# When the first six weight tiles of a fused Mamba and MLP kernel are loaded, and which products fill the second scan's norms

## The reference, cut to what matters

```python
h = patches @ W.T + b                       # tokens, 512 wide
x1 = layernorm(h)
r = x1 + mamba(rmsnorm(x1) * rms1_w)        # see below
r = r + down(silu(gate(n)) * up(n))         # n = rmsnorm(r) * rms2_w, hidden 2048
h = h + r
h = h + down2(silu(gate2(m)) * up2(m))      # m = layernorm(h), hidden 2048

# mamba, over the 10 tokens of one series, 1024 channels x 16 states:
z, xv, B, C, dt_in = split(x @ in_proj_w.T)
dt = softplus(dt_in @ dt_proj_w.T + dt_proj_b)
s[t] = exp(dt[t] * A) * s[t-1] + dt[t] * x[t] * B[t]
y[t] = sum over states of C[t] * s[t]
out = ((y + D_skip * x) * silu(z)) @ out_proj_w.T
```

## Time and profile before

| | |
|---|---|
| median of 3 runs | 665.3 us (664.75 to 665.99) |
| the profiled execution | 665.3 us, of which 663.5 us span |
| first scan, units 0 to 31 | about 30 to 203 us of the span |
| second scan, units 32 to 63 | about 203 to 440 us |
| outputs and MLPs of chunk 1 | from about 440 us |

### The profile page before, as it was taken

One profiled execution on the slowest core, in us unless ns is written; L12 is line 12 of the kernel. 1 busy time (PEld: TensorE's weight loads), 2 busy tenths in 40 slices (PEclk: granted clock), 3 DMA queues, 4 the chain that ended last, 5 costly groups with the idle time before them and its releaser, 6 DMA issues.

```text
span 663.5 us, 8621 instructions
## 1 busy us (share of the span) xinstructions
PE 627.1 (95%) x2846; PEld 501.8 (76%) x2846; DVE 416.9 (63%) x531; ACT 341.9 (52%) x768; POOL 429.0 (65%) x244
## 2 busy tenths in 40 slices
PE   5779998999995999999998999999999999999998
PEld 4547665666663767777765777766999998999998
DVE  4097887998877899888898888842232222332232
ACT  4368987488985564333374433413543443643440
POOL 0376766476777999987789987544465563455461
PEclk9959999999998999999999999999999999999999
DMA  8899996599999779988969998544244344244421
GB/s 334 305 372 344 304 328 231 189 356 347 329 362 395 279 250 367 412 332 308 323 223 312 402 326 315 171 127 159 96 133 151 103 154 127 66 144 136 131 68 44
DMA packets 49164, 163.50 MB, mean 246 GB/s; under 512 B 4320, under 2 KB 18528, under 8 KB 48480
## 3 DMA queue, kind: packets, MB, share of 16 engines
q1 hardware_dynamic: 49120, 162.95, 70.5%
HBM read 145.24 MB, written 17.69 MB: 246 GB/s over the span
## 4 chain that ended last, share of the span: by engine, by line
PE 76%; DVE 13%; issue 4%; ACT 3%; DMA 2%; POOL 1%; DVEq 0%; SPq 0%; ACTq 0%; POOLq 0%
PE work L1013 54%; PE da L1013 16%; DVE da L799 7%; PE work L1023 6%; DVE hs L809 3%; ACT L535 1%; DMA b_rows<-sq 1%; ACT da L561 1%; DMA bb<-b_rows 1%; DVE sq L883 1%; DMA sm<-small 1%; POOL hs L460 0%; DVE work L824 0%; DVE sq L899 0%; DVE a L892 0%
## 5 line engine op out<-in xcount | busy, mean ns | idle before, releaser
L799 DVE TENSOR_TENSOR_SCAN da<-da,hs 128x580 f32<-128x580 f32 (+1 forms) x128 | 191.1, 1493 | 35.0 <-POOL hs L460 19.2
L460 POOL TENSOR_TENSOR hs<-dtx,bb 128x1160 f32<-128x1160 f32 (+1 forms) x64 | 171.3, 2677 | 58.1 <-PE work L1023 43.7
L439 POOL TENSOR_TENSOR ws<-wraw,ws 128x1024 fp32r<-128x1024 f32 x40 | 101.3, 2534 | 92.9 <-ACT ws L570 92.9
L1013 PE MATMUL work<-sq,wraw 128*128 128x290 f32 x512 | 127.0, 407 | 3.8 <-DVE gate L952 2.6
L1013 PEld LDWEIGHTS work<-sq,wraw 128*128 128x128 f32 x512 | 96.1, 189 | 34.4 <-issue 4.8
L561 ACT ACTIVATE da<-dt,a_neg 128x261 f32<-128x261 f32 (+1 forms) x256 | 118.3, 494 | 0.0
L809 DVE TENSOR_TENSOR hs<-da,cb 128x580 f32<-128x580 f32 (+1 forms) x128 | 105.3, 823 | 15.3 <-DMA cb<-c_rows 6.8
L1013 PE MATMUL work<-hn,win 128*128 128x290 f32 (+1 forms) x336 | 98.7, 442 | 12.3 <-ACT c_rows L644 6.9
L1013 PEld LDWEIGHTS work<-hn,win 128*128 128x128 f32 x336 | 63.7, 192 | 41.9 <-issue 16.3
L558 ACT COPY da<-zeros 128x58 f32<-128x58 f32 (+1 forms) x128 | 27.7, 217 | 128.8 <-DVE hs L809 128.6
L570 ACT CAST ws<-wraw 128x1024 fp32r<-128x1024 f32 x48 | 50.3, 1049 | 70.4 <-PE da L1013 34.4
(11 more groups left out here) (103 smaller groups left out, 645.5 us busy)
## 6 DMA issues: line engine op xcount, KB each, us to landing
wraw<-w_stream SPq DMA_DIRECT2D x104, 512.0 KB, 4.0
bb<-b_rows SPq DMA_DIRECT2D x32, 700.0 KB, 7.5
cb<-c_rows SPq DMA_DIRECT2D x32, 700.0 KB, 5.9
bb<-b_rows SPq DMA_DIRECT2D x32, 580.0 KB, 8.5
cb<-c_rows SPq DMA_DIRECT2D x32, 580.0 KB, 6.7
c_rows<-c_rows SPq DMA_DIRECT2D x8, 875.0 KB, 10.6
c_rows<-c_rows SPq DMA_DIRECT2D x8, 725.0 KB, 7.1
win<-w_in SPq DMA_DIRECT2D x4, 1024.0 KB, 13.8
```

Of the source, the lines that this page charges most:

```text
L439: nc.gpsimd.tensor_tensor(ws[:, k % NW, 1, :], wraw[:, split_loads[k] % NRAW, :], ws[:, k % NW, 0, :].bitcast(F32), ALU.subtract).then_inc ...
L460: nc.gpsimd.tensor_tensor(hs[:, u % NH, 0:NQ * n].rearrange("p (n t) -> p n t", t=n), dtx[:, t % 2, 0:n].unsqueeze(1).to_broadcast([P, NQ, ...
L799: nc.vector.tensor_tensor_scan(da[:, j, 0:w], da[:, j, 0:w], hs[:, u % NH, j * w:(j + 1) * w], 0.0, ALU.mult, ALU.add).then_inc(scan_done, 1)
L1013: last = nc.tensor.matmul(dst, w, x, start=(k == 0), stop=(k == len(pairs) - 1))
```

## The change

Three things are changed. (1) The six first loads have a place each (`FIRST_LOADS`: the step beside which SP issues it, and the product that it waits for). Counted in units as SP reaches them: `wraw` 0 at unit 15, then 17, 18, 19, 24 and 25; before, all at unit 28. (2) `in_c` of tile 5 leaves unit 27 and is the filler ahead of `rms2`, in unit 36; `in_c` of tile 6 moves to the place behind `rms2`, which `in_z` of tile 7 had; and `in_z` of tile 7 goes to unit 33, ahead of the four outputs. (3) ACT loads the table with Tanh in the slots of `rms2` and `ln2_var`, at their end, where after `ln2_var` it was loaded just ahead of the first Tanh.

```diff
+FIRST_LOADS = [(("dtp", 0, 7), ("mean", 1)), (("in_x", 1, 1), ("in_x", 1, 0)), (("in_b", 1, 0), ("in_x", 1, 1)),
+               (("in_b", 1, 1), ("in_c", 1, 0)), (("in_z", 1, 0), ("in_z", 1, 0)), (("in_c", 1, 2), ("in_c", 1, 2))]
...
-    in_c = [("in_c", c, k) for k in (m, m + 1) if (c, k) != (0, 1)]
+    in_c = [("in_c", c, k) for k in (m, m + 1) if (c, k) not in ((0, 1), (1, 5))]
...
-    first = [[], [("xs", 1, 7)], o[0:2], o[2:4]]
+    first = [[], [("xs", 1, 7), ("in_z", 1, 7)], o[0:2], o[2:4]]
...
-        rest += {"rms2": [("in_c", 1, 6), s, ("in_z", 1, 7)], "ln2_mean": [s, ("dtp", 1, 7)],
+        rest += {"rms2": [("in_c", 1, 5), s, ("in_c", 1, 6)], "ln2_mean": [s, ("dtp", 1, 7)],
...
-SEAM = (("in_c", 1, 6), ("in_z", 1, 7), ("dtp", 1, 7), ("in_c", 1, 7))
+SEAM = (("in_c", 1, 5), ("in_c", 1, 6), ("dtp", 1, 7), ("in_c", 1, 7))
...
-                if i == 0:
-                    full(sp, ("in_z", 1, 2))
+                if i < NRAW:
+                    full(sp, FIRST_LOADS[i][1])
...
-                    if s == ("in_z", 1, 2):
-                        for i in range(NRAW):
+                    for i, (at, _) in enumerate(FIRST_LOADS):
+                        if s == at:
                             load_w(i)
...
                 if tables[0] == "silu_and_others" and unit is not None:
-                    use_tables("exp_and_others" if ("rms2", 0) in steps else "natural_log_exp_and_others")
+                    log_tables()
+                if ("rms2", 0) in steps or ("ln2_var", 0) in steps:
+                    if unit is not None:
+                        use_tables("exp_and_others")
```

## The result

The changed kernel takes 661.68 us (median of 6, 660.14 to 662.53) against 665.12 us beside it: ratio 0.9942, 95% interval 0.9928 to 0.9957, so 3.4 us less. The forecast was 662.3 us. Two later comparisons, on two chips, gave 0.9937 (0.9916 to 0.9957) and 0.9948 (0.9934 to 0.9962). The profiled execution took 661.63 us, of which 659.7 us span, 3.8 us less than the span before.

What follows compares the result with a forecast made beforehand. PE's chain was taken as the bound, held by a late last `y_done` as a load burst delayed DVE's rows. From 665.3 us, -4.0 + 1.3 + 0.6 - 0.95 = -3.05 us gave 662.3 us, range 659.0 to 665.6.

Steps and rivals of the forecast that it cites:

- The burst bounds the first scan's end: Near 200 us: six loads at once delay rows of C; without the burst the last `y_done` comes 4.0 us earlier.
- DVE keeps the whole of the 6.7 us: First scan's end: DVE gains all 6.7 us of its waits for C rows, giving 658.3 us; chance 0.13.
- the queue stays the bound: Up to the last `y_done`: rows still late by 2 to 3 us, about 664.8 us, no change; chance 0.17.
- `in_c` of tile 5 carries 0.7 us of it: First scan's end: removing this product from ahead of `in_z` carries about 0.7 of the 4.0 us gain.
- The early loads lose 1.3 us: Near 150 us: 3.8 us of backlog against 2.5 us of slack makes DVE wait 1.3 us for rows.
- The bounds of the step, 0 to 6.3: Early loads: 0 if DVE waits for ACT there anyway, 6.3 us if no slack covers anything.
- The second output waits 0.6 us longer: Outputs of chunk 0: its bank now awaits ACT's copy of the last `xs`, 6.6 us after `y_done`; 0.6 us lost.
- the clock gives nothing back, as PE waits for the bank instead: Outputs: 2.4 GHz held longer on PE gains 0 us, since the second output waits for its bank.
- The table at `ln2_var` gives 0.95 us: Seam at `ln2_var`: loading the table earlier, in ACT's idle time, brings Tanh, DVE and PE 0.95 us earlier.
- The store near 250 us costs nothing: Near 250 us: one more 875 KB store costs nothing, as rows have 4 us of lead against 3 us.
- The early loads cost more than they save: 126 to 180 us: five loads each hold the scan 1.3 us, giving 667.3 us, slower; chance 0.10.
- the clock falls late: Outputs: PE at 1.2 GHz for the first output and into the second, 2 us lost, 664.3 us; chance 0.08.

Runs made afterwards that it cites:

- loads_only: Only the six first loads moved, on the kernel before, with its products, banks and tables: ratio 0.9971, 664.26 against 666.45 us.
- late_table: Loads 1 to 5 at units 29 to 33 and the table moved, products as in the kernel before: ratio to before 0.9936, 660.72 us.
- loads_table: The six early loads and the table moved, products as in the kernel before: ratio 0.9967, 663.94 against 666.45 us.
- loads_table_again: Early loads and table moved, products as in the kernel before, repeated on another chip: ratio 0.9932, 660.91 against 665.33 us.
- banks: The changed kernel with the second, third and fourth output in banks 2, 0 and 1: 660.80 against its 661.95 us, ratio to before 0.9925.
- table_only: Only the `use_tables` lines of the diff, on the kernel before: ratio 0.9985, 665.47 against 666.45 us.
- order_only: Only the products and the banks that turn with them moved, on the kernel before, six loads still one burst: ratio 0.9980, 665.29 against 666.45 us.
- loads_late: The changed kernel with loads 1 to 5 at units 29 to 33 in place of 17 to 25: 660.70 against 661.95 us, ratio to before 0.9924.
- loads_late_again: The changed kernel with loads 1 to 5 at units 29 to 33, repeated on a third chip: 661.07 against 661.97 us, ratio to before 0.9938.
- banks_late: The changed kernel with outputs in banks 2, 0, 1 and loads 1 to 5 at units 29 to 33: 660.04 against 661.95 us, ratio to before 0.9904.

## Why the prediction was right, point by point

- **The burst bounds the first scan's end**: right, and shown by loads_only. Forecast 4.0 us earlier, measured 4.33 (7th to 8th multiplication). With the loss in between, the last `y_done` was to come at about 210.7 us and came at 209.84. The next bound is ACT, as worked out: DVE waits 1.74 us for the decays of unit 31, where 1.9 were named. As that stretch was 19.0 us in all seven profiles with the burst gone and the products moved, the rival in which DVE keeps all of its waits falls, and so does the one in which the queue stays the bound.
- **`in_c` of tile 5 carries 0.7 us of it**: right in size (late_table: 19.76 against 19.01), and the profiles sort by how far PE is ahead, not by how late DVE is. In loads_only PE began the three z 1.71 us ahead of the seventh multiplication, and the stretch was 19.00 us without the removal; in loads_table and loads_table_again it began them 0.83 and 0.92 us ahead, and the stretch was 19.76 and 19.67, though DVE was 3.7 us late in one and 0.8 in the other.
- **The early loads lose 1.3 us**: right in place, and mis-sized as a single number. DVE's waits for `cb` were 1.23 us in the first profile, of which 0.47 reached the seventh multiplication: a wait of 0.46 us that DVE had near there before is gone, and its waits for ACT are 0.15 us shorter. The larger wait (0.99 us) fell at unit 21, and only 0.24 at unit 23, whose slack the sum was made with. Seven profiles with early loads lost 0.5 to 3.7 us (median 0.9); seven without stay within 58.09 to 58.19 us. The bounds of the step, 0 to 6.3, held all of them, but are so wide that this says little: that the one number used lay near the measured ones is in part luck. The rule of the Trainium skill, "DMA: Bandwidth & Descriptors", section "Queues, rings and completion order", is that on each DMA engine a ring's descriptors are consumed in order. The rows agree in direction: those of C issued at 136.45 us, behind two loads, land 3.9 us later than before. By the prediction's 1.3 us for each load it would be 2.6, so in this execution that price was too low.
- **The second output waits 0.6 us longer**: measured 0.76 to the seam, and 1.0 against the clean pairs (30.45 against 29.45 in banks and 29.44 in late_table). The bank is the cause, by banks. The step "the clock gives nothing back, as PE waits for the bank instead" is also shown: the second output starts 6.6 us after the multiplication with the first at full clock (4.15 us) and at half clock (5.69 us), and in banks, with the wait gone, half clock takes part of the gain.
- **The table at `ln2_var` gives 0.95 us**: measured 1.03 in the profile and 1.0 by table_only.
- **The store near 250 us costs nothing**: from 239.83 to 346.62 us only the 1.03 us of the table differ.
- **The early loads cost more than they save** and **the clock falls late**, two of the rivals, did not come about in the changed kernel: 1.23 us of new waits and not 4.35, and the clock at 2.4 GHz behind both holes in its three profiles. Both came near in its neighbours: 5.27 us of waits in loads_only, of which 1.7 were lost, and two falls of the clock in order_only.
- The sum, -3.05 us, was 0.4 us short of the medians' 3.4. In the profile two terms were mis-sized towards too slow, by 0.3 and 0.8 us, and the rest took back 0.4: the scan was 0.34 us late from its start, which no term held, and the bank cost 0.16 more, the table gave 0.08 more.

What stays open is why the same early loads cost 0.5 us in one execution and 3.7 in another. The profiles show the waits for `cb` at units 21 to 25 in changing places, in two of them one more near 183 us, with a DMA share of 1.03 to 1.04 from 130 to 155 us in each; no run told what sets them. A part of the 3.7 us goes with the half clock behind PE's wait in loads_table, where DVE waits 1.33 us for PE in two places; how much it makes in sum isn't separated. It was not tried whether the chips differ in it: for the one on which loads and table gave only 0.9967 no run of the full change is on record.

## What to carry to other kernels

A prefetch that nobody needs for 30 us is not free when its queue is full: what counts is the lead of the transfers behind it, and how much the queue has to carry there without it. Six tiles at once used up a lead of 3 to 7 us. One tile per unit cost 0.5 us and more where the share was 1.04 already (130 to 155 us), and nothing from 185 to 205 us, where it was 0.94 without them (the changed kernel) and 1.02 with them (loads_late). When steps move between slots, the rotation of PSUM banks moves with them, and a product may come to wait for a copy that nobody waited for; it is read from the order of the banks before the run.

## What the runs showed of the hardware that was not expected

The length of a hole on PE doesn't tell whether the clock falls. Ahead of the outputs the granted clock stayed at 2.4 GHz with holes of 2.72, 2.84 and 2.72 us (the changed kernel) and 2.73 us (loads_late), and fell to 1.2 GHz with 2.72 us (loads_late_again, the same kernel as loads_late), 2.73 us (banks_late) and 2.92 us (banks). With shorter ones it fell too: 2.31 us, twice, in order_only and 2.29 us in loads_table, while the waits of 2.46 us behind the first output left it alone. In banks and banks_late it was back at 2.4 GHz some 4 us after the products began.

The lead of a transfer in a full queue is not a fixed number from one execution to the next: without early loads the stretch of 58.1 us repeats within 0.1 us, and with them it varies by 3.2 us (58.63 to 61.88 us; the longest has the fall of the clock in it).
